# Scores from 32-row groups of TensorE on the keys as they are, and other PSUM banks for shifted scores and weighted values

## The reference, cut to what matters

```
B, S, D, H = (4, 256, 128, 16)      # DK = D // H = 8
q = split_heads(layernorm(x) @ Wq + bq); k = split_heads(ctx @ Wk + bk); v = split_heads(ctx @ Wv + bv)
scores = einsum('bhqd,bhkd->bhqk', q, k) / sqrt(DK)
scores = where(mask == 0, -1e9, scores)
x = x + (softmax(scores) @ v, heads joined) @ Wo + bo
```

## Time and profile before

| | us |
|---|---|
| median of 3 runs (lowest, highest) | 250.22 (249.75, 250.79) |
| time of the profiled execution | 252.34 |
| its span, first to last instruction | 250.5 |
| mean granted TensorE clock, share of full | 0.944 |
| busy: TensorE 193.8, VectorE 185.7, ScalarE 135.1, GpSimd 117.5 | |

### The profile page before, as it was taken

How to read it: one execution, slowest core, us unless ns; L and a number is a source line. 1 busy time by engine, 2 the same in 40 slices (tenths; PEclk the granted TensorE clock), 3 DMA queues, 4 the chain that set the end, 5 groups by cost and what they waited for, 6 DMA issues and landing times.

```text
span 250.5 us, 4608 instructions
## 1 busy us (share of the span) xinstructions
PE 193.8 (77%) x1654; PEld 125.8 (50%) x1654; DVE 185.7 (74%) x456; ACT 135.1 (54%) x271; POOL 117.5 (47%) x231
## 2 busy tenths in 40 slices
PE   0389866998628588777999879979879987999950
PEld 0268654797512277552334435434537865666420
DVE  4579888877684979879766868858355349499996
ACT  2136744838676578436677658658790654431000
POOL 8131768996539767811788784782040020000000
PEclk9999998699975789999999999999997999999996
DMA  5994040000000000000000000000000000000000
GB/s 171 338 395 191 0 167 4 0 4 0 4 0 0 0 0 3 3 3 3 0 0 5 1 3 0 0 3 0 3 1 3 0 3 0 1 3 21 21 21 21
DMA packets 4460, 8.73 MB, mean 35 GB/s; under 512 B 514, under 2 KB 3026, under 8 KB 4052
## 3 DMA queue, kind: packets, MB, share of 16 engines
q1 hardware_dynamic: 3636, 7.78, 8.3%
q10 hardware_dynamic: 800, 0.63, 0.9%
HBM read 7.88 MB, written 0.52 MB: 34 GB/s over the span
## 4 chain that ended last, share of the span: by engine, by line
PE 28%; POOL 28%; DVE 20%; issue 11%; ACT 8%; DMA 3%; SPq 1%; POOLq 0%; DVEq 0%
PE ps L1229 25%; POOL gate_pt L511 6%; POOL rstd L377 5%; POOL w L397 3%; PE ps L1238 3%; POOL x_in L428 3%; DMA wf<-weights_dram 3%; POOL w L389 2%; DVE mx L1082 2%; DVE gate_pt L1025 2%; DVE amax L1019 2%; DVE stats L794 2%; ACT gate_pt L754 2%; POOL vareps L374 2%; POOL spread L498 2%
## 5 line engine op out<-in xcount | busy, mean ns | idle before, releaser
L1082 DVE TENSOR_REDUCE mx<-ps 128x2 f32<-128x512 f32 x64 | 42.0, 686 | 15.6 <-PE ps L1229 15.5
L754 ACT ACTIVATE gate_pt<-ps 128x512 f32<-128x512 f32 x64 | 37.0, 603 | 15.2 <-PE ps L1229 14.9
L511 POOL TENSOR_SCALAR gate_pt<-ka 32x256 f16<-32x256 f16 x64 | 25.5, 399 | 4.4
L1229 PE MATMUL ps<-gate_pt,half_c 128*128 128x512 f16 x64 | 24.1, 379 | 3.3 <-issue 1.9
L1229 PE MATMUL ps<-qb,gate_pt 128*128 128x256 f16 x128 | 24.6, 274 | 1.0 <-ACT gate_pt L754 0.2
L1229 PE MATMUL ps<-gate_pt,hid_xm 128*32 128x256 f32 x256 | 20.4, 390 | 1.5 <-ACT gate_pt L754 1.5
L1229 PE MATMUL ps<-w,half_c 128*128 128x512 f16 x96 | 21.2, 379 | 0.0
L1238 PE MATMUL ps<-cst,rows 128*128 128x128 f32 x32 | 8.0, 351 | 13.9 <-ACT rows L659 6.6
L1229 PEld LDWEIGHTS ps<-qb,gate_pt 128*128 128x128 f16 x128 | 9.1, 97 | 18.5 <-issue 10.6
L377 POOL TENSOR_TENSOR rstd<-vareps,halfs 128x2 f32<-128x2 f32 x24 | 17.0, 710 | 2.0
L498 POOL TENSOR_SCALAR spread<-mx 128x16 f16<-128x16 f32 x32 | 5.9, 201 | 23.9 <-DVE mx L1082 17.6
(11 more groups left out here) (221 smaller groups left out, 523.7 us busy)
## 6 DMA issues: line engine op xcount, KB each, us to landing
stage<-weights_dram SPq DMA_DIRECT2D x2, 1024.0 KB, 10.8
wf<-weights_dram SPq DMA_DIRECT2D x4, 256.0 KB, 8.6
wf<-mask_dram SPq DMA_DIRECT2D x1, 1024.0 KB, 4.6
eb_oT<-ffw_dram SPq DMA_DIRECT2D x1, 768.0 KB, 8.7
ctx_in<-ctx_rows_dram ACTq DMA_DIRECT2D x4, 128.0 KB, 6.4
x_in<-x_dram SPq DMA_DIRECT2D x4, 128.0 KB, 3.0
gate_pt<-ctx_cols_dram SPq DMA_DIRECT2D x1, 512.0 KB, 8.4
out_dram<-ctx_in SPq DMA_DIRECT2D x4, 128.0 KB, 1.7
```

The lines of the kernel that those rows point to most:

```text
L511: ins = nc.gpsimd.tensor_scalar(kz[part, n % KRING, k], ka[part, b, quad], 1.0, 0.0, ALU.mult, ALU.add)
L754: nc_act(pt[:, head % PRING].rearrange("p t n -> p (t n)"), ps[:, 2 + head % 2, :], ACT.Exp, scale=DK ** -0.5).then_inc(sig["probs"], 1)
L1082: V.tensor_reduce(mx[:, b, head:head + 2, t], score_bank(4 * n + i).rearrange("p (h n) -> p h n", h=2), AX.X, ALU.max).then_inc(sig["smax" ...
L1229: return nc.tensor.matmul(dst, lhsT, rhs, start=start, stop=stop, skip_group_check=True)
```

## The change

- The separated keys go: no `kz`, no memset of it, none of the 64 copies on GpSimd. Plain and shifted scores contract over the head's own 32 rows: `mm(dst, qa[head rows], ka[head rows])` and `mm(dst, ka[head rows], qb[head rows])`.
- Plain scores are made by head: two matmuls of 256 columns (the two token tiles) in place of one of 512; `head_max` reads the same 512 columns of a bank. The heads come in the order 2, 3, 0, 1 (`PLAIN_HEADS`).
- The two token tiles of shifted (n, k) and plain (n+2, k) are issued alternately: shifted t0, plain t0, shifted t1, plain t1. Both waits (for the bank of the shifted and of the plain scores) stand ahead of the four.
- Shifted scores have three banks in turn (2, 3, 5): they wait for the exponential three heads before.
- Weighted values have bank 4 alone: those of an even quad wait until the two quads before are copied away (`oT`). `out_copy` stands behind the exponential of k = 2 of an even quad, in place of behind k = 3.

```diff
-KRING = 4
+PLAIN_HEADS = (2, 3, 0, 1)
+SHIFTED_BANKS = (2, 3, 5)
+VALUES_BANK = 4
...
+        def shifted_bank(head):
+            return ps[:, SHIFTED_BANKS[head % len(SHIFTED_BANKS)], :]
...
-            pool.wait_ge(sig["kscale"], 1)
-            nc.gpsimd.memset(kz[:, :, :, :], 0.0).then_inc(sig["zeros_ready"], 1)
...
-            def separated_keys(n):
...
-                    ins = nc.gpsimd.tensor_scalar(kz[part, n % KRING, k], ka[part, b, quad], 1.0, 0.0, ALU.mult, ALU.add)
...
-                if n + KRING < B * QUADS:
-                    pool.wait_ge(sig["spread"], n + 3)
-                    separated_keys(n + KRING)
-                    pool.wait_ge(sig["kz_ready"], n + KRING + 1)
...
-                nc_act(oT[...], ps[:, 4 + m % 2, :], ACT.Copy)
+                nc_act(oT[...], ps[:, VALUES_BANK, :], ACT.Copy)
...
-                if n >= 2 and n % 2 == 0:
-                    out_copy(n // 2 - 1)
+                    if n >= 2 and n % 2 == 0 and k == 2:
+                        out_copy(n // 2 - 1)
...
+            def scores_tile(n, i, t, masked):
+                b, quad = divmod(n, QUADS)
+                head = rows_of(PLAIN_HEADS[i])
+                dst = score_bank(i)[:, t * T:(t + 1) * T]
+                ins = mm(dst, qa[head, b, quad, t * P:(t + 1) * P], ka[head, b, quad], True, not masked)
...
+            def shifted_wait(n, k):
+                head = 4 * n + k
+                if k == 0:
+                    pe.wait_ge(sig["qb"], n + 1)
+                if head >= len(SHIFTED_BANKS):
+                    pe.wait_ge(sig["probs"], head - len(SHIFTED_BANKS) + 1)
...
+            def shifted_tile(n, k, t, masked):
+                b, quad = divmod(n, QUADS)
+                tok = slice(t * P, (t + 1) * P)
+                dst = shifted_bank(4 * n + k)[:, t * T:(t + 1) * T]
+                ins = mm(dst, ka[rows_of(k), b, quad, tok], qb[rows_of(k), n % 2], True, not masked)
...
+            def shifted_beside_plain(n, k, masked):
+                shifted_wait(n, k)
+                plain = n + 2 < B * QUADS
+                if plain:
+                    scores_wait(n + 2, k)
+                for t in range(TILES):
+                    shifted_tile(n, k, t, masked)
+                    if plain:
+                        scores_tile(n + 2, k, t, masked)
...
-                    if m >= 2 and n % 2 == 0:
-                        pe.wait_ge(sig["oT"], m - 1)
+                    if m and n % 2 == 0:
+                        pe.wait_ge(sig["oT"], m)
```

More of the change, by code:

```diff
@@ L502, in shift_rows @@
                 ins.then_inc(sig["spread"], 1)
-            def separated_keys(n):
[L505 to L510, removed]
-                    ins = nc.gpsimd.tensor_scalar(kz[part, n % KRING, k], ka[part, b, quad], 1.0, 0.0, ALU.mult, ALU.add)
-                ins.then_inc(sig["kz_ready"], 1)
-            pool.wait_ge(sig["zeros_ready"], 3)
+            pool.wait_ge(sig["zeros_ready"], 2)
             pool.wait_ge(sig["ln_rstd"], nth_norm(LN_ATT, B - 1))
-            for n in range(KRING):
-                separated_keys(n)
-            pool.wait_ge(sig["kz_ready"], KRING)
             shift_rows(0)
@@ L707, in out_copy @@
                 b, half = divmod(m, 2)
[L708 removed]
+                nc_act(oT[:, b, 2 * half:2 * half + 2].rearrange("p h n -> p (h n)"), ps[:, VALUES_BANK, :], ACT.Copy)\
                     .then_inc(sig["oT"], 1)
@@ L1078, in head_max @@
                 b, quad = divmod(n, QUADS)
-                t, pair_of = divmod(i, 2)
-                head = 4 * quad + 2 * pair_of
+                head = 4 * quad + PLAIN_HEADS[i]
                 dve.wait_ge(sig["s_mm"], 4 * n + i + 1)
-                V.tensor_reduce(mx[:, b, head:head + 2, t], score_bank(4 * n + i).rearrange("p (h n) -> p h n", h=2),
+                V.tensor_reduce(mx[:, b, head, :], score_bank(i).rearrange("p (t n) -> p t n", t=TILES),
                                 AX.X, ALU.max).then_inc(sig["smax"], 1)
@@ L1445, in queries, with rows_of, scores_wait, scores @@
                 ins.then_inc(sig["q_mm"], 1)
-            def scores(n, i, masked):
+            def rows_of(k):
+                return slice(32 * k, 32 * k + 32)
+            def scores_wait(n, i):
                 b, quad = divmod(n, QUADS)
-                t, pair_of = divmod(i, 2)
                 if n == 0 and i == 0:
                     pe.wait_ge(sig["qa_ready"], 1)
-                if i == 0:
-                    pe.wait_ge(sig["kz_ready"], n + 1)
+                if quad == 0 and i == 0:
+                    pe.wait_ge(sig["ka_ready"], B + b + 1)
                 if 4 * n + i >= 2:
                     pe.wait_ge(sig["smax"], 4 * n + i - 1)
-                dst = score_bank(4 * n + i)
-                ins = mm(dst, qa[:, b, quad, t * P:(t + 1) * P],
-                         kz[:, n % KRING, 2 * pair_of:2 * pair_of + 2].rearrange("p h n -> p (h n)"), True, not masked)
-                if masked:
-                    for h in range(2):
-                        ins = mm(dst[:, h * T:(h + 1) * T], idbig[:, :], resmask[:, b, t], False, h == 1)
-                ins.then_inc(sig["s_mm"], 1)
+            def scores_tile(n, i, t, masked):
[3 more added lines that the diff above has]
+                ins = mm(dst, qa[head, b, quad, t * P:(t + 1) * P], ka[head, b, quad], True, not masked)
+                if masked:
+                    ins = mm(dst, idbig[:, :], resmask[:, b, t], False, True)
+                if t == TILES - 1:
+                    ins.then_inc(sig["s_mm"], 1)
+            def scores(n, i, masked):
+                scores_wait(n, i)
+                for t in range(TILES):
+                    scores_tile(n, i, t, masked)
             def shift(n):
@@ L1473, in shift @@
                 mm(ps[:, 6, 0:T], id16[:, :], qa[:, b, quad], False, True).then_inc(sig["shift_mm"], 1)
-            def shifted_scores(n, k, masked):
-                b, quad = divmod(n, QUADS)
+            def shifted_wait(n, k):
                 head = 4 * n + k
@@ L1480, in shifted_scores @@
                     pe.wait_ge(sig["qb"], n + 1)
-                if head >= 2:
-                    pe.wait_ge(sig["probs"], head - 1)
-                for t in range(TILES):
[L1484 to L1491, removed]
+                if head >= len(SHIFTED_BANKS):
[5 more added lines that the diff above has]
+                ins = mm(dst, ka[rows_of(k), b, quad, tok], qb[rows_of(k), n % 2], True, not masked)
+                if masked:
+                    for q in range(TILES):
+                        ins = mm(dst[:, q * P:(q + 1) * P], resmask[:, b, q, tok], idbig[:, :], False, q == TILES - 1)
+                if t == TILES - 1:
+                    ins.then_inc(sig["st_mm"], 1)
+            def shifted_beside_plain(n, k, masked):
[3 more added lines that the diff above has]
+                    scores_wait(n + 2, k)
+                for t in range(TILES):
+                    shifted_tile(n, k, t, masked)
+                    if plain:
+                        scores_tile(n + 2, k, t, masked)
             def weighted_values(n, t):
@@ L1587, in attention @@
                     for k in range(4):
-                        shifted_scores(n, k, masked)
-                        if n + 2 < B * QUADS:
-                            scores(n + 2, k, masked)
+                        shifted_beside_plain(n, k, masked)
                         if k == 1 and n + 1 < B * QUADS:
```

8 lines of the change are left out of this document (3 added, 5 removed).

## The result

| | before | changed |
|---|---|---|
| median of 4 runs each (lowest, highest), us | 250.2 (249.75, 250.79) | 259.44 (255.81, 262.67) |
| time of the profiled execution; its span | 252.34; 250.5 | 262.67; 260.7 |
| granted TensorE clock of the profiled execution | 0.944 | 0.861 |

The changed kernel is slower: ratio 1.0267, interval 1.0212 to 1.0322. That ratio, like the ratios with an interval in the experiments, compares the less disturbed runs of each kernel (here 255.8 to 257.6 us) and leaves out the others (261.6 to 265.3 us), though their cause is the same one. The plain medians stand 1.037 to one another. The forecast was 246.2 us, range 242.3 to 252.5: wrong, and on the wrong side.

The account below looks back on a forecast made before the run. Four engines stood close together, so the 3.71 us loop turn was taken as the bound, at full clock. Terms -3.0 - 2.1 + 1.1 = -4.0 took 252.34 to 248.3, less 2.1 for the median: 246.2 us, range 242.3 to 252.5.

Parts of the forecast that it names:

- TensorE's clock falls: Rival for the whole attention: 1.2 GHz in place of 2.4, 13 x 1.9 = 25 us lost, 271 us; chance 0.06.
- The price per turn: In that clock rival, TensorE's 1.9 us of each turn's path double at 1.2 GHz, over 13 turns.
- Row groups overlap: In the loop's scores, the four matmuls of one k take 0.22 us in place of 0.44; no-overlap rival's chance 0.15.
- Odd turns: Loop turns of odd quads 1 to 13: 3.41 us in place of 3.71, 2.1 us gained over seven.
- Even turns: Loop turns of even quads 2 to 12: the bank copy makes them 3.89 us against 3.71, 1.1 us lost over six.
- GpSimd's copies: In the attention, dropping the key copies frees late shifts (0.84) and layer-norm roots (2.2): -3.0 us together.
- Drains of the tail steps: At k = 2 and 3, nine tail steps drain TensorE 2.2 us, 0 on the path; drains rival, 250.2 us, chance 0.12.
- After the attention: Behind the loop nothing changes; if the clock dip there goes or lasts longer, 1.1 us either way.

Follow-up runs that it names:

- e12: e9 with its start fillers reading 32 rows in place of 128, those of turn 0 into free bank 5; 262.26 us, ratio 1.0103, 1.042 over all twelve runs.
- e1: The change with its 32-row groups and interleaving, but the banks and the place of out_copy of the kernel before; 256.39 us (252.52 to 263.16).
- e9: e1 with pairs of full-row filler matmuls only at the attention's thin start and behind each k of turn 0; 250.52 us, ratio 0.9981.
- e13: e9 with three fillers at its places in place of two, and two behind k = 3 of later turns and in the last two; 248.15 us, ratio 0.9826.
- e3: The kernel before with 48 of GpSimd's 64 key copies left out, later quads using stale keys; 248.73 us, ratio 0.9921.
- e2: The kernel before with only the change's banks (three shifted, one for weighted values) and its place of out_copy; 252.77 us, ratio 1.0052.
- e5: The change with two shifted banks (2, 3) and two 128-row filler matmuls into bank 5 behind each k of the loop; 269.9 us.
- e8: The change with two shifted banks (2, 3) and three 128-row filler matmuls into bank 5 behind k = 2 and 3 alone; 271.66 us.
- e15: e13's kernel run once more, on the chip of the kernel before with e13's fillers; 247.04 us, ratio 0.9839.
- e7: The change with plain heads in the order 0, 1, 2, 3, so shifted and plain scores of one k share a row group; 287.97 us, ratio 1.143.

## Why the prediction was wrong

**The step that failed** is that the sum left TensorE's clock at 1.00 through the attention, with the rival "TensorE's clock falls" at a chance of 0.06. The argument against it was that the weighted values, full of small pieces, did not lower the clock. These work on all 128 rows and 32 columns, and they are 0.57 of a turn of 3.71; the new matmuls work on 32 rows. I took one kind of small matmul for the other. I also priced it as all or nothing (271 us). It is neither: in the profiled run TensorE was at 1.2 GHz for 44 us of 75, and in other runs for other shares. The price per turn was near: 1.9 forecast; an even turn takes 5.37 for 3.84, 1.53 more, and in e12, with the banks of before, four turns of both parities take 5.15 or 5.16 for 3.41, 1.75 more. An estimate from these: 44 us are 8.2 turns at 1.53 or 8.5 at 1.75, 12.6 to 15.0 us; the 10.6 measured leave -2.0 to -4.4 for all the rest, where the sum had -4.0 and the terms as measured below give -2.0 - 1.2 - 0.3 = -3.5. So without the fall the forecast would have been near. The windows that bounded the kernel showed a clock of 1.00, and I worked with it as a constant of the kernel instead of as a result of the work that the change replaces.

The other terms, by their steps:

- *Row groups overlap*, 0.22 per k: right. Shifted and plain start 0.00 to 0.02 apart, and even four row groups of two k at once, which I had not thought of. By the Trainium skill, "TensorE: Matmul & The Clock Gate", Part 3, matmuls in different row groups run concurrently; the trace agrees (four starts from 127.68 to 127.69).
- *Odd turns* 3.41, -2.1 for seven: the walk right, 3.41 in e1, e9, e13; the sum too large. Against e3, which has GpSimd's copies gone and full-row scores, the odd turns at 1.00 in e1, e9 and e13 give 0.28, 0.28, 0.30, 0.12, 0.17, 0.12 and in the last nothing, 1.2 in all: only turns without other waits win the whole.
- *Even turns* 3.89, +1.1 for six: the walk right, 3.84 in the change; the sum wrong in sign. With two values banks an even turn takes 3.41 too (e1), and against e3 all six win some 0.27, 1.6 in all. The single bank takes 0.43 of that back at n = 4 and 12 and nothing at n = 10, the even turns that the change ran at 1.00. An estimate, if n = 8 goes with the first two and n = 2 and 6 with the last, as in e2: -1.6 + 1.3 = -0.3.
- *GpSimd's copies* -3.0: the mechanism right, the size -2.0 (e3). I had counted each root's 1.11 in full, and 0.74 of it reaches the turn; and one turn then waits 0.50 longer for VectorE.
- *Drains of the tail steps*, 0 on the path: nothing speaks against it, as e1's turns around tail steps at 1.00 (4.13, 4.65, 4.48, 4.94) are shorter than those of e3 in the same places (4.43, 4.91, 4.60, 5.11). Not tested alone.
- *After the attention*: unchanged but for where the fall at its end lies.

What stays open: why the clock falls at one place in one run and not in the next of the same kernel; why it stays down for 40 us under full-row fillers in e5 and e8; and how many rows would do, as no kernel with 64 rows was tried.

## What to carry to other kernels

Before matmuls over the full array are replaced by ones over 32 rows, look at the granted clock of the stretch and price the stretch at both levels: here the row groups win some 4 us once the clock is held (e13 and e15, with the banks of before), and the change loses 10 with 44 us at 1.2. If the structure wins otherwise, put a few full-row matmuls where TensorE waits anyway, above all where the stretch begins thinly, and measure many runs, for the mean then depends on how often the clock holds. Fillers in the wrong place cost double: they run at the lower level themselves.

## What was not expected of the hardware

- TensorE busy 4.1 to 5.0 of every 5 us stays at 1.2 GHz for 99 us (e7), when most of that work is on 32 rows.
- In the kernel before, the keys of the scores are zeros in 96 of the 128 rows, and the clock stands at 1.00 from 105 to 188 us. Zeros in those rows did not cost the clock; leaving the rows out did.
- The levels are sticky: e5 and e8, with the same fillers throughout, ran some 40 us at 0.50 and then, from 156 and 161 us, at 1.00 to the end of the attention.
- The same kernel differs by 6% between runs on one chip (e9: 248.87 to 264.54 us), where the kernel before keeps within 2%.
- Matmuls of two successive k, four row groups, start within 0.01 us, and the next follow 0.18 later (127.68 to 127.86, at 1.2 GHz, where one alone takes 0.21 in e7), so the cost of a row-group matmul can drop below half of a full one.
